# Attention with routed experts: the attention order of four engines, the first norm on ScalarE, and a memset between GpSimd's transfers

## The reference

```python
x = x + xattn(layernorm(x), ctx, ctx, W_q, b_q, W_k, b_k, W_v, b_v, W_o, b_o, mask)
x = x + ffn(layernorm(x), Wp, sim_matrix, temperature, W1, b1, W2, b2)
# xattn
scores = einsum('bhqd,bhkd->bhqk', qh, kh) / sqrt(d_k)
scores = where(mask == 0, -inf, scores)
attn = softmax(scores, axis=-1)
context = einsum('bhqk,bhkd->bhqd', attn, vh)
# ffn
pn, sn = l2norm(x @ Wp.T), l2norm(sim_matrix)
top_v, top_i = top_k(pn @ sn.T / temperature, 2)
comb = sum(one_hot(top_i, E) * softmax(top_v)[..., None], axis=-2)
h = gelu(einsum('bsd,edf->ebsf', x, W1) + b1, approximate=False)
eo = einsum('ebsf,efd->ebsd', h, W2) + b2
out = einsum('ebsd,bse->bsd', eo, comb)
```

## Time and profile before

| what | us |
|---|---|
| median of three runs | 445.17 (445.03 to 445.3) |
| the profiled execution, its own time | 443.8 |
| its span, first to last instruction | 442.0 |
| mean granted TensorE clock | 0.948 |

### The profile page before, as it was taken

How to read it: one execution, slowest core, us unless ns; L and a number is a source line. 1 busy time by engine, 2 the same in 40 slices (tenths; PEclk the granted TensorE clock), 3 DMA queues, 4 the chain that set the end, 5 groups by cost and what they waited for, 6 DMA issues and landing times.

```text
span 442.0 us, 13885 instructions
## 1 busy us (share of the span) xinstructions
PE 359.1 (81%) x3564; PEld 299.5 (68%) x3565; DVE 310.4 (70%) x970; ACT 284.6 (64%) x815; POOL 268.3 (61%) x427
## 2 busy tenths in 40 slices
PE   3869888988897889888977878949869999989900
PEld 2447766665675667566755768949769999989900
DVE  5257989888988898889878555635546555556872
ACT  3458887878787878777877465725436565656531
POOL 5623367767686778776863345565655655556673
PEclk9969999999999999999999599978989999999965
DMA  6900001101110101012000032222212222129463
GB/s 172 371 1 5 20 27 40 44 28 33 32 43 24 31 31 43 24 31 82 27 26 14 19 76 56 57 61 63 68 51 67 64 68 61 54 61 264 119 173 113
DMA packets 39052, 29.24 MB, mean 66 GB/s; under 512 B 5107, under 2 KB 34751, under 8 KB 39008
## 3 DMA queue, kind: packets, MB, share of 16 engines
q1 hardware_dynamic: 30592, 18.33, 14.5%
q0 software_dynamic: 4384, 8.60, 6.2%
q10 hardware_dynamic: 4032, 1.77, 1.4%
HBM read 17.53 MB, written 11.62 MB: 66 GB/s over the span
## 4 chain that ended last, share of the span: by engine, by line
PE 59%; DVE 19%; issue 10%; SPq 4%; another core or an unknown queue 2%; DVEq 2%; ACT 1%; DMA 1%; POOL 1%; ACTq 0%; POOLq 0%
PE ps_s L902 14%; PE ps_s L891 13%; PE ps_o L654 8%; PE ps_t L643 6%; PE ps_s L627 5%; DVE rows L1248 5%; DVE sums L1180 3%; SPq L346 3%; PE ps_o L662 2%; PE ps_o L724 2%; PE ps_s L617 2%; PE ps_x L674 2%; DVE pr L1174 2%; DVE cxT L1197 1%
## 5 line engine op out<-in xcount | busy, mean ns | idle before, releaser
L561 POOL DMA_INDIRECT results<-eo,didx x71 | 70.6, 995 | 64.6 <-issue 34.4
L446 POOL DMA_INDIRECT lists<-rows,slots x64 | 65.4, 1021 | 47.8 <-DVE slots L1313 34.1
L891 PE MATMUL ps_s<-xtT,w1c 128*128 128x128 f32 x568 | 78.8, 283 | 7.5 <-DVE xtT L1576 5.5
L948 ACT ACTIVATE pT<-ps_t 77x512 f32<-77x512 f32 x128 | 72.2, 589 | 19.2 <-PE ps_t L643 17.4
L891 PEld LDWEIGHTS ps_s<-xtT,w1c 128*128 128x128 f32 x568 | 70.6, 195 | 12.4 <-DVE xtT L1576 10.0
L902 PE MATMUL ps_s<-w2s,hT 128*128 x568 | 77.5, 281 | 0.6 <-ACT hT L1108 0.4
L643 PE MATMUL ps_t<-identf,pr 128*77 128x128 f32 x512 | 74.5, 286 | 0.0
L902 PEld LDWEIGHTS ps_s<-w2s,hT 128*128 128x128 f32 x568 | 70.4, 195 | 1.2 <-issue 1.0
L1108 ACT ACTIVATE hT<-h 128x512 f32<-128x512 f32 x71 | 44.7, 629 | 39.2 <-PE ps_s L902 25.4
L1104 ACT ACTIVATE w1c<-w1s 128x512 f32 x71 | 44.8, 631 | 34.3 <-PE ps_s L891 16.7
L643 PEld LDWEIGHTS ps_t<-identf,pr 128*77 128x77 f32 x512 | 61.7, 154 | 6.5 <-issue 4.1
(11 more groups left out here) (204 smaller groups left out, 607.6 us busy)
## 6 DMA issues: line engine op xcount, KB each, us to landing
xt<-lists SPq DMA_DIRECT2D x71, 66.0 KB
ys<-results SPq DMA_DIRECT2D x16, 256.0 KB, 4.5
xin<-in_x_dram SPq DMA_DIRECT2D x16, 128.0 KB, 2.2
w1s<-in_L_ffn_W_dram SPq DMA_DIRECT2D x1, 2048.0 KB, 10.0
out_dram<-x ACTq DMA_DIRECT2D x6, 256.0 KB
cin<-in_ctx_dram SPq DMA_DIRECT2D x16, 77.0 KB
results<-eo,didx POOLq DMA_INDIRECT x71
lists<-rows,slots POOLq DMA_INDIRECT x64
```

The source lines that it names most:

```text
L446: nc.gpsimd.indirect_dma_start(lists, bass.IndirectOffsetOnAxis(ap=slots[:, r, s * TOPK + k:s * TOPK + k + 1], axis=0), rows[:, r, s, k, : ...
L561: nc.gpsimd.indirect_dma_start(results, bass.IndirectOffsetOnAxis(ap=didx[:, r:r + 1], axis=0), eo[:, r, :], None, bounds_check=TOPK * NTO ...
L891: last = nc.tensor.matmul(ps_s[:, r, c * P:(c + 1) * P], w1c[:, r, c * P:(c + 1) * P], xtT[:, r, :], start=True, stop=True)
L948: nc.scalar.activation(pT[0:SK, g, :], ps_t[0:SK, g % 2, :], ACT.Copy).then_inc(E[f"t{g}_ready"], 1)
```

## The change

It writes the attention programs of PE, ACT, DVE and POOL in another order, with other offsets between the engines. The first norm goes from POOL to ACT: POOL makes `nmean` (-mean) and `shift1` (-mean times rstd), two instructions of 128x2 more, and ACT computes x * rstd + shift. The four scatters of a pair stand apart. Pair 14 is routed to its end in the attention stage (`NP - 1` in place of `NP - 2` in the conditions), and pair 15's routing is put nearer to the start of the expert stage (its scatters at tiles 8 to 11). In the expert stage POOL executes a memset of 128x416 behind each indirect transfer. At the end 11 sequences in place of 8 are added between the last tiles, ACT loads the last chunk, stores only chunks 0 to 2 and can go on to weigh; SP stores the other five.

```diff
-    DRAINED = 20
+    DRAINED = 9
+    LOOPED = DRAINED + 18
-    EARLY = 8
+    EARLY = 11
+    LATER = 3
+        pace = sb("pace", [P, 2, 416])
@@ SP @@
-            all_returned(N_TILES)
-            for c in range(PART // CH, NB // CH):
-                load_results(c)
-
-            for c in range(PART // CH, NB // CH):
+            all_returned(sp, N_TILES)
+            load_results(sp, PART // CH)
+
+            for c in range(LATER, NB // CH):
                 store(sp, c)
@@ POOL, first_power @@
+                nc.gpsimd.tensor_scalar(nmean[:, :], mv1[:, r, :, 0], -1.0, 1.0, ALU.mult, ALU.mult).then_inc(E["nm1"], 1)
                 nc.gpsimd.tensor_scalar(ve1[:, :], mv1[:, r, :, 1], LN_EPS, 1.0, ALU.add, ALU.mult).then_inc(E["var1"], 1)
...
+                nc.gpsimd.tensor_tensor(shift1[:, r, :], nmean[:, :], rstd1[:, r, :], ALU.mult).then_inc(E["sh1"], 1)
-            def first_norm(J, m):
...
-                for s in range(2):
-                    last = nc.gpsimd.tensor_scalar(xn[:, s, :], xin[:, r, s, :], mv1[:, r, s, 0:1], rstd1[:, r, s:s + 1],
-                                                   ALU.subtract, ALU.mult)
@@ POOL, give_back @@
                 after_tile(pool, FE["eo_ready"], j)
+                after_tile(pool, FE["paced"], j - 2)
                 settled(pool)
                 nc.gpsimd.indirect_dma_start(results, bass.IndirectOffsetOnAxis(ap=didx[:, r:r + 1], axis=0),
                                              eo[:, r, :], None, bounds_check=TOPK * NTOK - 1, oob_is_err=False
                                              ).then_inc(returned[r], 16)
+                nc.gpsimd.memset(pace[:, m % 2, :], 0.0).then_inc(FE["paced"], 1)
@@ POOL, between @@
-                if j == 9:
+                if j == 1:
                     gate_power(NP - 1, NP - 1)
-                elif 10 <= j < 14:
-                    scatter(NP - 2, NP - 2, (j - 10) // TOPK, [(j - 10) % TOPK])
-                elif 21 <= j < 25:
-                    scatter(NP - 1, NP - 1, (j - 21) // TOPK, [(j - 21) % TOPK])
+                elif 8 <= j < 12:
+                    scatter(NP - 1, NP - 1, (j - 8) // TOPK, (j - 8) % TOPK)
@@ ACT @@
+            def first_norm(J, m):
+
+                r = m % 2
+                after(act, E["sh1"], J)
+                after(act, E["xT_done"], J - 1)
+                for s in range(2):
+                    last = nc.scalar.activation(xn[:, s, :], xin[:, r, s, :], ACT.Identity, bias=shift1[:, r, s:s + 1],
+                                                scale=rstd1[:, r, s:s + 1])
+                last.then_inc(E["xn_ready"], 1)
...
-            for c in range(PART // CH):
+            all_returned(act, N_TILES)
+            for c in range(PART // CH + 1, NB // CH):
+                load_results(act, c)
+            for c in range(LATER):
                 store(act, c)
@@ DVE, step: of the whole new order, the neighbours of second_norm @@
-                if has(J, -1):
-                    sum_most(J - 1, m - 1, 1)
-                if has(J, -2, NP - 1):
-                    second_norm(J - 2, m - 2)
...
+                if has(J, -2):
+                    reciprocals_wide(J - 2)
...
+                if has(J, -3, NP - 1):
+                    second_norm(J - 3, m - 3)
```

More of the change, by code:

```diff
@@ L872, in _ @@
             pe.wait_ge(wpt_copied, 2)
[L873 removed]
+            steps(pe, step, 1, 18, 6, 14)
             pe.wait_ge(tab_ready, 3)
@@ L1645, in _ @@
             for c in range(EARLY // CH, NB // CH):
-                mine = [b for b in range(c * CH, (c + 1) * CH) if not on_pool(b)]
+                mine = [b for b in range(c * CH, (c + 1) * CH) if b >= EARLY and not on_pool(b)]
                 after_y(dve, c)
```

457 lines of the change are left out of this document (224 added, 233 removed).

## The result

The changed kernel takes **426.66 us** (median of four runs, 425.26 to 428.4) against 445.21 us of the kernel before on the same chip: a ratio of 0.9586, 95% interval 0.9549 to 0.9622. The forecast was 417.1 us with a range of 405 to 434. The profiled execution took 427.02 us, against 443.8 before, so 16.8 us are gone where 28.1 were expected.

The account below looks back on a forecast made before the run. No single engine was taken as the bound; waits between engines set the attention step and slowed the expert stage. Terms -16.6 + 3 - 12 - 2.5 = -28.1 took 443.8 to 415.7, plus 1.4 gave 417.1 us, range 405 to 434.

Parts of the forecast that it names:

- Second norm beside the keys: Attention: DVE's second norm, held by POOL's key multiplication, would finish before it starts, -1.03 us a step.
- Scatters apart: Attention: spacing POOL's scatters would remove a third of the 1.07 us by which the values end late, -0.35 us.
- First norm to ACT: Attention: ACT's busy time would rise from 11.53 to 12.30 us a step, still under PE's 12.39; nothing charged.
- The step: Attention: a step would fall from 14.58 to 13.2 us, over about 12 full steps -16.6 us.
- the step does not shorten: Rival, attention: the norm meets another POOL operation, or ACT makes the waits anew; 433.7 us, chance 13%.
- One more step: Attention's end: a further partial step in DVE's and PE's programs, with pair 14's routing in it, costs +3 us.
- Memset: Expert stage: 0.43 us more behind each POOL transfer stops transfers going in pairs 1.37 us apart, saving 6 us.
- Pair 14's and 15's scatters: Expert stage: one group of scatters in place of two keeps 7 of about 15 us lost, plus 3 for routing waits.
- End: Kernel's end: ACT no longer waits for later stores and DVE has fewer sequences left, -2.5 us.
- Spacing buys nothing: Rival, expert stage: late signals have another cause and the stage stays at 155 us; 429.1 us, chance 17%.
- The memset never waited for DVE: Judges a rival, expert stage: memset held on the shared port by 1.03 us each time, 472 us, chance 4%.
- ACT is on the chain of the step: Judges a rival, attention: late `shift1` delays ACT, a step takes 16 us; 450.7 us, chance 3%.

Follow-up runs that it names:

- before_scatters_apart: Kernel before with only the four scatters of a pair in the attention stage set apart, other POOL work between them: 453.06 us, ratio 0.9979 to the kernel before.
- pace_scatters: Changed kernel with a 128x416 memset also behind each of pair 15's four scatters at tiles 8 to 11: 421.34 us, ratio 0.9434 to the kernel before.
- spread_scatters: Changed kernel with pair 15's four scatters at tiles 8, 11, 14 and 17, not 8 to 11: 421.54 us, ratio 0.9477 to the kernel before.
- both: Changed kernel with pair 15's scatters at tiles 8, 11, 14, 17 and a memset behind each: 414.18 us, ratio 0.9997 to the kernel before.
- act_more: Changed kernel with one more 128x128 copy, unused, on ACT behind the first norm in each step: 430.04 us, ratio 0.9548 to the kernel before.

## Why the prediction was right, and where not

The time lies in the range, 9.6 us above the point; on the profiled executions it is 427.0 for 415.7, 11.3 above. By the steps of the forecast, on the profiled executions:

- **Second norm beside the keys (-1.03 a step).** The mechanism is right: 1432 ns became 410, and where the copy `recx` met the keys instead, it was held by 0.8 to 1.1 us. The size is not: done alone the edit gave 0.42. Of a delay that lay on the chain 0.39 us came back further on, on DVE behind the second maxima.
- **Scatters apart (-0.35).** In the change the late values are charged 1.49 in place of 2.15, 0.66 less, and 0.41 are left, beside a single scatter. In `before_scatters_apart` the late ends are gone but for one in seven. So the direction is right, though a single scatter is enough there for a part. The one run that made the edit alone put waits of its own in its place, so the size is not shown; the third chip, where no end is late, has steps 0.2 to 0.3 us shorter.
- **First norm to ACT (nothing charged).** This is the step that failed as far as is known. The norm was costed at nothing because ACT's busy sum stayed under PE's, and that sum was right, even high (12.00 for 12.30). But busy time added to ACT at this place has a price of about 1 to 1 in the new step (0.20 us more, 0.21 longer), because it stands in the stretch in which PE waits for ACT, 0.72 us a step. Late values explain at most a part of the missing 0.64 us: on the third chip none is late, and the step is still 0.3 to 0.4 over the forecast's 13.2. That the step would be shorter without the norm on ACT isn't shown; the run that took it away made a ring elsewhere.
- **The step (-16.6).** 13.84 and not 13.2. The last sum moved by 9.6 us. The rival "the step does not shorten" had named ACT, and was half true.
- **One more step (+3).** 5.9 us were given back between last sum and first tile, near the upper bound of 7. A lower granted clock (0.77 for 0.89) is part of it; which wait holds it was not tried. These 2.9 us and the 7.0 of the step are most of the 11.3.
- **Memset (-6 for the pairs).** 0.46 us for 0.43, distances of 1.76 for 1.80, no pairs. Alone on the kernel before it gave 6.7; taken from the change it cost 11.0. Of these only 0.2 lie at the scatters (tiles 8 to 14 take 19.3 us without and 19.1 with it). The rest is the pairs again: with one place of scatters in place of two, more tiles are left that can pair up, and 56 x 0.19 = 10.6.
- **Pair 14's and 15's scatters (-6).** One place is left, of 6.9 us, for an estimate of 7. The stage is 142.7 us for 143, but the 7 were a share of a sum for which no mechanism was given, so that they fit is in part luck. That it was not a price of the scatters but of their distance, and could be had back with four more memsets, the forecast did not see: it counted POOL's lag there as a cost, and the tiles stayed at 1.9 us with a lag of 7.3.
- **End (-2.5).** -0.6. ACT no longer waits for its stores, as expected, but the end is set by the last transfer back and the load behind it, 2.16 and 5.59 us, and the first starts later for the memsets. The term looked at who waited before, not at what is late next.
- **The rivals.** "Spacing buys nothing" is refuted on the chip of the first group (435.0 us without, 421.3 with the most of it). The rule of the Trainium skill that DMA never contends with a compute engine ("SBUF — State Buffer", "Who interferes with whom") holds in these traces for the instructions themselves: the values take 1.08 us on PE whether their end is late or not. What the forecast drew from it, that thinning out transfers helps no engine, does not hold on that chip, and does on the third. The memset never waited for DVE: 458 to 488 ns, 71 times. ACT is on the chain of the step, at 13.84 us and not at 16.

The terms as measured are -9.6 + 5.9 - 12.4 - 0.6 = -16.7 us; the spans differ by 16.8.

**The better version.** `pace_scatters` and `spread_scatters` beat both kernels: 0.9434 and 0.9477 of the kernel before, where the change has 0.9586; their intervals lie below the change's, but that was not measured beside them. `both` was only run on the third chip, where it equals the kernel before.

## What to carry to other kernels

Where engines wait for signals of instructions that took no longer than usual, look at where GpSimd's indirect transfers start and how near they are to each other, and space them, with idle work or by moving one; then check it on more than one chip, since the loss was not on each. Price a moved operation by the stretch in which it will stand on its new engine: if another engine waits for that stretch, what it adds to the busy time there can cost as much, whatever the busy sum says, and one added copy shows it. A delay taken off a chain can come back in part further on, and an operation also counts by the buffer that it frees.

## What the runs showed of the hardware that was not expected

- Indirect transfers of GpSimd in turn 1.63 and 1.35 us apart go with three tiles in 12.64 us in the change (and 12.47 in `act_more`, on the chip of the second group); 1.63 and 1.73 apart, on the chip of the first group, with 5.71. On the chip of the third group the same 1.34 apart cost nothing (5.70), and the kernel before reads 414.16 us there against 445.21, 446.5 and 450.52. What differs between the chips no run tells.
- VectorE beside GpSimd's key multiplication (two tiles read, 1.22 us): a norm of 0.40 us takes up to 1.43, a copy of 0.29 up to 1.35. Beside GpSimd's first norm (one tile read, 0.80 us each) two norms take 0.79 to 0.91 us in place of 0.73.
- An `activation` with scale and bias read from SBUF takes 0.49 us for 128x128, the scaled copy of the earlier trace rows 0.385, a plain copy 0.306 (292 to 308 ns, 16 times, in `act_more`). In a row they overlap: that copy adds 0.20 us of busy time.
- A memset of 128x416 takes 0.458 us and was never held by VectorE's work on the experts, which reads from PSUM.
